# Two tiles through the weights together, ten rows of counts a tile, and the next row's bases loaded behind a row's first addition

## The reference

```python
def rgcn_conv(x, edge_index, edge_type, W_rel, W_root, bias):
    src, dst = edge_index
    h_src, out = x[src], x @ W_root + bias
    for r in range(2):
        w = (edge_type == r)
        sums = segment_sum(h_src @ W_rel[r] * w[:, None], dst, N)
        cnt = segment_sum(w, dst, N)
        out = out + sums / maximum(cnt, 1.0)[:, None]
    return out
# layer 0: x + elu(rgcn_conv(t5_norm(x), ...)) @ wo, then x = layernorm(x + that)
# layer 1: layernorm, 1024 -> 512 -> 256, three rounds of
#   h = h + relu(layernorm(relu((h + segment_sum(h[src], dst)) @ Wa + ba) @ Wb + bb)),
#   decoder 256 -> 512 -> 1024, residual and two layernorms
```

## Time and profile before

| | |
|---|---|
| median of 3 runs | 574.75 us (574.73 to 575.24) |
| the profiled execution's own time | 576.75 us |
| its span | 574.9 us |
| mean granted TensorE clock | 0.992 |
| busy: PE, DVE, ACT, POOL | 97%, 65%, 42%, 18% of the span |

### The profile page before, as it was taken

The page is one execution under the profiler, slowest core; times in us unless marked ns, Lnnn a source line. Parts: engine busy times, 40 slices in busy tenths (PEclk is TensorE's granted clock), DMA queues, the critical chain, the costliest instruction groups (busy, mean ns, idle before and its releaser), DMA issues.

```text
span 574.9 us, 8853 instructions
## 1 busy us (share of the span) xinstructions
PE 556.9 (97%) x2708; PEld 399.4 (69%) x2708; DVE 371.8 (65%) x1070; ACT 243.5 (42%) x484; POOL 101.7 (18%) x80
## 2 busy tenths in 40 slices
PE   6999999999999999999999999999999999999992
PEld 3655555555588989888889888868868867555541
DVE  7588898888838889887430230048658667855555
ACT  3363465636565464653222121023232233366555
POOL 4010000000000000020444532202202230132230
PEclk8999999999999999999999999999999999999998
DMA  8511011111031211238200001500100100022123
GB/s 265 151 31 27 22 36 36 36 36 36 2 93 37 72 38 45 64 102 231 112 2 0 0 0 29 201 1 1 38 0 0 37 0 2 0 73 65 42 72 107
DMA packets 20963, 30.77 MB, mean 54 GB/s; under 512 B 5458, under 2 KB 15404, under 8 KB 20928
## 3 DMA queue, kind: packets, MB, share of 16 engines
q1 hardware_dynamic: 20512, 29.66, 17.4%
q10 hardware_dynamic: 416, 0.67, 0.4%
HBM read 25.20 MB, written 5.12 MB: 53 GB/s over the span
## 4 chain that ended last, share of the span: by engine, by line
PE 77%; DVE 9%; DVEq 5%; issue 5%; DMA 2%; ACT 1%; POOL 0%; SPq 0%
PE banks L991 12%; PE banks L1077 12%; PE banks L906 12%; PE banks L781 8%; PE banks L874 5%; PE banks L1013 5%; PE banks L1003 4%; PE banks L939 4%; PE banks L941 4%; DVEq L1253 3%; PE banks L1067 3%; DVE cnt L1261 2%; PE banks L916 2%; DVE oh_both L1241 2%; DVE oh_both L1236 1%
## 5 line engine op out<-in xcount | busy, mean ns | idle before, releaser
L781 PE MATMUL banks<-w_all,xnT 128*125 128x429 f32 x320 | 133.4, 541 | 2.5 <-DMA w_all<-in_L_gnn_W_rel 2.5
L781 PEld LDWEIGHTS banks<-w_all,xnT 128*125 128x125 f32 x320 | 54.6, 190 | 32.6 <-issue 32.6
L906 PE MATMUL banks<-hT,w_s 128*128 128x250 f32 x320 | 68.9, 375 | 0.1
L906 PEld LDWEIGHTS banks<-hT,w_s 128*128 128x128 f32 x320 | 60.2, 189 | 8.5 <-issue 1.4
L939 PE MATMUL banks<-y_hi,adj 125*125 125x288 f32 x200 | 55.2, 303 | 0.3 <-issue 0.3
L1261 DVE TENSOR_TENSOR cnt<-cnt,banks 125x110 f32 x160 | 42.6, 266 | 18.1 <-issue 12.6
L941 PE MATMUL banks<-y_lo,adj 125*125 125x286 f32 x200 | 53.5, 294 | 0.0
L991 PE MATMUL banks<-adj,h_hi 125*128 125x250 f32 (+1 forms) x180 | 48.3, 367 | 0.3 <-issue 0.2
L1408 DVE TENSOR_SCALAR hT<-banks,g_c,b_c 128x125 f32<-128x125 f32 x60 | 19.4, 401 | 45.1 <-PE banks L891 45.0
L759 PEld LDWEIGHTS banks<-oh_both,oh_low 125*128 125x128 bf16 x320 | 23.2, 98 | 34.9 <-issue 20.1
L991 PE MATMUL banks<-adj,h_lo 125*128 125x250 f32 (+1 forms) x180 | 45.7, 353 | 0.0
(11 more groups left out here) (224 smaller groups left out, 943.5 us busy)
## 6 DMA issues: line engine op xcount, KB each, us to landing
xt<-in_x SPq DMA_DIRECT2D x15, 448.0 KB
out_x<-ot SPq DMA_DIRECT2D x9, 448.0 KB
w_s<-in_L_gnn_W SPq DMA_DIRECT2D x5, 512.0 KB, 6.4
xn<-in_x SPq DMA_DIRECT2D x5, 448.0 KB
wd_s<-in_L_gnn_Wd SPq DMA_DIRECT2D x1, 2048.0 KB, 11.9
w_all<-in_L_gnn_W_rel SPq DMA_DIRECT2D x6, 286.0 KB, 6.6
wo_s<-in_L_gnn_wo_weight SPq DMA_DIRECT2D x1, 1024.0 KB, 6.2
w_all<-in_L_gnn_W_root SPq DMA_DIRECT2D x3, 286.0 KB, 5.9
```

Of the source, the lines that this page charges most:

```text
L781: ins = pe.matmul(pb[0:P, 2 + 2 * v + n, 0:FH], xnT[:, u], w_all[:, u, n * FH:(n + 1) * FH], start=(u == 0), stop=(u == KD - 1))
L906: ins = pe.matmul(pb[:, b0 if f == 0 else 4 + f % 2, 0:2 * P], w1_s[:, k, f * 128:(f + 1) * 128], hT[:, k], start=(k == 0), stop=(k == KD ...
```

## The change

Four things. (1) Tiles 0 and 1 are projected together: for each pair of blocks u, tile 0's products are followed by tile 1's, from a second buffer `xnT1`; SP loads tile 1's x behind the second piece of the weights, and the three edge lists go from ScalarE's queue to SP's, behind the third piece. The transposes of the edges move behind later products, and those of tile 2's first half stand ahead of tile 0's last two blocks. (2) `tile_of_1` runs for tiles 2 to 9 and has UG = 10 rows each, with two rows ahead of the first product and two ahead of the fifth. (3) The counts are split at the columns 0, 300, 600, 900 and 1060 instead of every 250. (4) On DVE the load of the next row's bases stands behind a row's first addition instead of behind its weighing.

```diff
-DONE = 2 * P
+DONE = 300
+PARTED = (0, DONE, 2 * DONE, 3 * DONE, 1060, N)
-UG = KD + 1
+UG = KD + 2
...
-            for q in range(len(PIECES)):
-                load_w(sp, q)
+            load_w(sp, 0)
+            load_w(sp, 1)
             load_x(1, 1)
+            load_w(sp, 2)
+            for a, d, done in ((dst_i, dst, dst_in), (src_i, src, src_in), (typ_i, typ, typ_in)):
+                sp.dma_start(a[:], d.rearrange("(g e) -> g e", g=G)).then_inc(done, 16)
+            load_w(sp, 3)
+            load_w(sp, 4)
...
+            def weigh_blocks(t, turned):
+
+                for k in range(KD):
+                    act.wait_ge(xnT_ps, 1 + 2 * t + k // 4)
+                    act.activation(turned[:, k], pb[:, 6 + k // 4, k % 4 * P:(k % 4 + 1) * P], ACT.Copy,
+                                   scale=lnw[:, k:k + 1]).then_inc(first_turned, 1)
+
+            weigh_blocks(0, xnT)
             squares(0, 0)
             root_of(0, 0)
+            weigh_blocks(1, xnT1)
+            squares(1, 1)
+            root_of(1, 1)
+            act.wait_ge(xs_in[0], 64)
+            act.wait_ge(xn_rstd, 1)
+            squares(2, 0)
+            root_of(2, 0)
...
-            def tile_of_1(t, v, g0, odd, rows, uses):
+            def tile_of_1(t, v, g0, uses):
...
                 for u in range(KD):
-                    row(u if u <= 4 else u + extra)
+                    row(u + (u > 0) + (u > 4))
                     if u == 0:
                         pe.wait_ge(xnT_copied, 1 + t * 2)
                         turn(1, v)
+                        row(1)
...
-                        if extra:
-                            row(5)
+                        row(6)
                     products(u, v)
...
+            def first_products(u, t):
+
+                pe.wait_ge(first_turned, KD * t + u + 1)
+                for n in range(2):
+                    ins = pe.matmul(pb[0:P, 2 + 2 * t + n, 0:FH], (xnT, xnT1)[t][:, u], w_all[:, u, n * FH:(n + 1) * FH],
+                                    start=(u == 0), stop=(u == KD - 1))
+                if u in (3, KD - 1):
+                    ins.then_inc(proj_mm, 1)
+
+            for u0 in range(0, KD, 2):
+                for t in range(2):
+                    if t == 1 and u0 == 0:
+                        pe.wait_ge(xs_in[1], 32)
+                        pe.wait_ge(first_turned, KD)
+                        turn(0, 1)
+                        turn(1, 1)
+                    if t == 1 and u0 == 2:
...
+                    if t == 1 and u0 == 4:
...
+                        turn_edges(0, e_low)
+                        turn_edges(7, e_val)
+                        turn_edges(1, e_code).then_inc(edges_ps, 1)
+                    if t == 0 and u0 == 6:
+                        pe.wait_ge(xs_in[0], 64)
+                        turn(0, 0)
+                    for u in (u0, u0 + 1):
...
+                        first_products(u, t)
...
-            def tile_of_1(t, v, g0, odd, rows, placed):
+            def tile_of_1(t, v, g0, placed):
 
                 base = bases(g0)
-                for u in range(rows):
+                for u in range(UG):
...
                     place(base, b, 0, placed, first_added)
-                    more = rows == UG or u + 2 < rows
-                    if more:
-                        codes(g + 2, b).then_inc(codes_set, 1)
-                        lows(g + 2, b)
+                    now = base
+                    if u + 1 < UG:
+                        base = bases(g + 1)
+                    codes(g + 2, b).then_inc(codes_set, 1)
+                    lows(g + 2, b)
                     dve.wait_ge(first_added, g + 1)
-                    place(base, b, 1, placed, counts_free)
-                    if more:
-                        weighed_codes(g + 2, b).then_inc(onehots, 1)
-                    if u + 1 < rows:
-                        base = bases(g + 1)
+                    place(now, b, 1, placed, counts_free)
+                    weighed_codes(g + 2, b).then_inc(onehots, 1)
```

More of the change, by code:

```diff
@@ L433, in _ @@
         def _(act):
-            for s in (xnT_copied, y_copied, hT_lo, r1_done, d1_done):
+            for s in (xnT_copied, xnT_copied, xnT_copied, xnT_copied, xnT_copied, y_copied, hT_lo, r1_done, d1_done):
                 act.sem_inc(s, 1)
@@ L496, in tile_of_1 @@
                 if complete is not None:
-                    act.wait_ge(counts_free, complete * (2 * UG) + 2 * UG + 2)
-                    part(complete, bass.ds(complete * DONE, DONE))
+                    k, cols, rows = complete
+                    act.wait_ge(counts_free, rows + 2)
+                    part(k, cols)
                 evacuate(t, v)
@@ L532, in _ @@
+            tile_of_1(T - 2, 0, 32 * (T // 2), False, None, (2, slice(PARTED[2], PARTED[3]), 6 * UG))
+            tile_of_1(T - 1, 1, None, True, None, (3, slice(PARTED[3], PARTED[4]), 7 * UG))
             act.wait_ge(counts_free, G + 2)
-            part(T // 2 - 1, slice(N - DONE, N))
+            part(4, slice(PARTED[4], N))
             def elu_parts_of(t):
@@ L823, in _ @@
             turn(1, 0)
[L824 to L849, removed]
+            warm(1, 5)
@@ new lines, in first_products @@
+            def first_products(u, t):
[13 more added lines that the diff above has]
+                    if t == 1 and u0 == 2:
+                        pe.wait_ge(bounds_ready, 1)
+                        for i in range(2 * H):
+                            ins = pe.transpose(pb[0:1, i // H, i % H * G:(i % H + 1) * G], bounds[:, i:i + 1], ident[0:G, 0:G])
+                        ins.then_inc(bounds_ps, 1)
+                    if t == 1 and u0 == 4:
+                        pe.wait_ge(lows_ready, 1)
+                        pe.wait_ge(edges_ready, 1)
+                        pe.wait_ge(prep, 9)
+                        pe.wait_ge(first_turned, 2 * KD)
+                        turn_edges(0, e_low)
[5 more added lines that the diff above has]
+                    for u in (u0, u0 + 1):
+                        for q, ks in enumerate(PIECES):
+                            if u == ks[0] and t == 0:
+                                pe.wait_ge(w_in[q], 48)
+                        first_products(u, t)
@@ L850, in _ @@
             pe.wait_ge(codes_ready, 1)
             pe.wait_ge(far_copied, 2)
[L852 to L854 removed]
+            with pe.Fori(0, T // 2 - 2) as i:
+                tile_of_1(i * 2 + 2, 0, i * (2 * UG), i * 32 + 64)
+                tile_of_1(i * 2 + 3, 1, i * (2 * UG) + UG, i * 32 + 96)
             pe.wait_ge(big_ready, 1)
@@ L927, in relations @@
                         pe.wait_ge(pre_elu, t - 1)
-                    if t % 2 == 0:
-                        pe.wait_ge(parted, t // 2 + 1)
+                    pe.wait_ge(parted, sum(c0 < (t + 1) * P for c0 in PARTED[:-1]))
                     b = 2 * (t % 2)
```

65 lines of the change are left out of this document (30 added, 35 removed).

## The result

The changed kernel takes 611.9 us at the median (611.2 to 612.6, 4 runs) against 575.0; the ratio is 1.063, 95% interval 1.060 to 1.065. The forecast was 606, the range 598 to 614. The profiled execution spans 610.8 us, 35.9 more than before; the forecast of this sum was 31.7.

The account below looks back on a forecast made before the run. PE and DVE were taken as both full in the counting stage, DVE bounding after the change. First addition 37.9 plus stage 153.4 plus 0.5 gives 191.8 against 160.07, so +31.7 on 574.75: 606 us, range 598 to 614.

Parts of the forecast that it names:

- The row, 1.86 us: DVE's row in the counting stage: load behind the first addition delays the codes, making the row 0.30 us longer than 1.56.
- The stage from row 0's first addition to the aggregation, 153.9 us: Eight tiles at 19.3 us on DVE, less 0.6 for the end: 153.4, plus 0.5 for weighing and flag.
- The opening, first addition at 37.9: Start of kernel: row 0's first addition moves from 25.68 by +13.0 for tile 1's work and -0.8 for the lists.
- 0.8 us for the lists: Opening: edge lists moved behind the weights leave 0.48 MB less ahead of them, worth 0 to 2.1 us; 0.8 taken.
- the slow passes: Opening on PE: the first eight passes take 4.81 us, eight later ones 2.93, at a granted clock of 0.89.
- Afterwards nothing changes: From the aggregation's start, at 191.8 us, the rest of the kernel was to be unchanged, making +31.7 us in all.
- rival C: PE's clock falls to 1.2 GHz in the counting stage: up to +86 us, 692 for the whole stage; chance 0.03.
- PE waits in pieces of under 1.5 us: Argument against a clock fall in the counting stage; the earlier fall came after 2.5 us of idle.
- Rival A: Load hidden in its new place: DVE's row 1.30 us, PE bounds at 15.0 a tile, about 573 us; chance 0.07.
- Rival B: Load costs the same in its new place: DVE's row 1.56 us, tile 16.7, total 587 us; chance 0.06.
- What would show it: Signs: DVE idle about 0.5 us before codes, rows 1.86 apart, tiles near 19 us, PE busy near 78%.
- Both engines are full: Counting stage before the change: PE and DVE each need 14.8 us per nine-row tile, no room for a tenth row.

Follow-up runs that it names:

- the pair load: Changed kernel with the load back behind the weighing, but one load of four registers brings two rows' bases, behind odd rows' weighing: 572.7 us, ratio 0.9947.
- loop written out, new place: Changed kernel, load still behind the first addition, with DVE's loop over tile pairs written out so waits and addresses are constants: 591.8 us, ratio 1.028.
- pair load in the new place: Changed kernel with one four-register load for two rows, placed behind the odd rows' first addition: 580.7 us, ratio 1.008.

## Why the prediction was right

The forecast of 606 missed the median by 6 us, within its range. Part of that closeness is luck: in the sum of the profiled executions, 35.9 us against 31.7, the stage is 5.8 longer than worked out, the rest behind it 1.4 longer, and the opening 3.0 shorter. The remainder lies in the executions profiled, which were 2.0 us over the median before and 0.7 after. The cause it named is shown from both sides: the load put back takes 26 us away, the load moved alone adds 24. Point by point:

- *The row, 1.86 us.* It is 1.92. The step is right in kind: weighing 0.18, next first addition 0.47 (worked out 0.48) behind the second addition. The gap from first addition to codes was taken as 0.75 and is 0.80. Over the 64 rows that were taken at 1.86 this makes 3.5 to 3.8 us, the larger part of the stage's 5.8. By the floor of about 600 ns that the Trainium skill gives for the load ("DMA: Bandwidth & Descriptors", table of latencies) the sum would have been nearer, 612; but the loads lasted 0.52 to 0.55 us in the changed kernel, so that is chance, and the measurement decides.
- *The stage from row 0's first addition to the aggregation, 153.9 us.* It is 159.7. Beside the row, one row in each tile has more than 0.54 us idle ahead of the codes: 0.93 and 0.89 in the first two tiles (codes at 51.59 and 69.48), 0.64 to 0.67 in the six later ones (as at 91.35), some 1.4 us in all. What it is stays open; in the run with the load back there are 0.26 and 0.23 us at such places in the first two tiles and none later, and there the sequencer's next step comes late without a wait. The last 0.5 us lie at the border: from the last second addition (193.06) to the aggregation are 1.5 us, where the sum has 1.0. Of them 1.0 stand between the start of DVE's flag (193.57) and the first matmul; before the change it was 1.1 (158.99 and 160.07).
- *The opening, first addition at 37.9.* It came at 34.85, so 3.0 us of the error were hidden by one the other way. I took 0.8 us for the lists and kept the slow passes. The first products came 2.3 us earlier and ran at full clock. In the run with the lists back the late start and the slow passes return together (8.93, 4.84 us, 0.94 over the stretch). But the run with only the load moved, with the opening of before, had no slow passes and its first addition at 23.68. So up to 2.0 us of the 25.68 from which I counted belonged to that one execution and not to the kernel. Tile 1's x was waited for 0.15 us, and the edges' preparation ended at 19.56 (19 worked out), hidden as said.
- *Afterwards nothing changes.* Not quite: +1.4 us. I had looked for the clock (rival C) inside the stage, where the granted clock stayed at 1.00; it fell at the end of it, behind 2.22 us of idle. "PE waits in pieces of under 1.5 us" had left out that border, though the sum itself has DVE end last there.
- *Rival A* would have given 573, and did (573.5) where the loads were taken out. *Rival B*, 587 with an unchanged row, is what the load back in its place shows: 586.0. *Rival C* did not come about in the stage.
- *What would show it.* Idle 0.5 ahead of the codes (0.54), none ahead of the first addition, the load in the chain: all there. A tile was to take 19.3 us and takes 19.8 on the mean. PE busy near 78% of the stage: 83%.
- *The fuller account of the bound.* "Both engines are full" holds for the kernel before with PE as the one that counts: PE was idle for 1.3 us of the stage, so DVE's idle of 0.18 a row can have cost no more than that. With ten rows a tile DVE became the bound: at the old row the stage costs 11 us more, and with a shorter one (the pair load) it costs nothing.

## What to carry to other kernels

In all runs here a load into registers was executed by DVE's in-order sequencer and delayed what stood behind it, not what had been handed over ahead of it. Put it where most handed-over work is still to run, behind the last instruction that needs no more waiting, and not behind the first one that had to wait; count from single starts what is queued there. And before an engine gets more rows a tile, work out its row with the idle that busy shares leave out.

## What the runs showed of the hardware

- The length of DVE's register load depends on how many it brings and from where: two registers 0.52 to 0.55 us from even and odd rows alike, four from a row that starts at a multiple of 16 bytes from the array's start 0.34 to 0.38, four from one 8 bytes off 0.96 to 0.98. Other offsets and numbers were not tried.
- With that, the best version here is the changed kernel with one aligned load for two rows in the old place: 572.7 us, 0.5% under the kernel before. PE is busy for 119.44 us of 120 in its stage (35 to 155), so hardly more is to be had there from DVE.
- A wait of some 2 us at a border between stages can cost nearly as much again. In the changed kernel PE was idle for 2.22 us; then the granted clock was 0.50, the lower of the two levels, in the stretch from 196, and the rest of the kernel took 1.4 us longer. The same border in the other traces: behind 1.97 us of idle (the lists ahead), 2.04 and 2.11 (four registers every row, new and old place) and 2.29 (loop written out, new place) the clock fell to 0.50 as well; behind 1.79 (only the load moved), 1.60 (pair load in the new place), 1.45 (load back) and less it stayed at 1.00. At the start of the kernel 2.50 us (the kernel before) and 2.12 (the lists ahead) were followed by about half clock, 1.39 (only the load moved) was not. The written-out kernel's stretches, same columns as above:

```profile
175.00:177.00 2.00, 1.97 (x13) 2.00 (x14) 0.00 (x0) 1.97 (x2) 1.16 (x1) 0.88 0.87 75
177.00:179.00 2.00, 2.00 (x11) 2.00 (x10) 0.00 (x0) 1.98 (x2) 0.00 (x0) 0.50 0.88 318
179.00:181.00 2.00, 2.00 (x13) 2.00 (x13) 0.62 (x2) 0.70 (x1) 0.00 (x0) 0.76 0.67 229
```
